# Second cross attention: two head pairs per output product with values as weights, sums of keys on GpSimd, maxima in a bank of their own

## The reference, cut to what matters

```python
def _L1_xattn_ref(x, y, Wq, Wk, Wv, Wp, bp):
    # x: layernorm of the rows (8, 64, 512), y: ctx_1024 (8, 1601, 512), H, D = 16, 32
    q = (x @ Wq.T).reshape(B, N, H, D)
    k = (y @ Wk.T).reshape(B, L, H, D)
    v = (y @ Wv.T).reshape(B, L, H, D)
    attn = jnp.einsum('bnhd,blhd->bhnl', q, k)
    attn = jax.nn.softmax(SCALE * attn, axis=-1)
    out = jnp.einsum('bhnl,blhd->bnhd', attn, v).reshape(B, N, C)
    return out @ Wp.T + bp
```

## Time and profile before

| | us |
|---|---|
| median of 3 runs | 1368.89 (1365.0 to 1373.93) |
| the profiled execution | 1376.89 |
| its span in the trace | 1375.2 |

### The profile page before, as it was taken

How to read it: one execution, slowest core, us unless ns; L and a number is a source line. 1 busy time by engine, 2 the same in 40 slices (tenths; PEclk the granted TensorE clock), 3 DMA queues, 4 the chain that set the end, 5 groups by cost and what they waited for, 6 DMA issues and landing times.

```text
span 1375.2 us, 34061 instructions
## 1 busy us (share of the span) xinstructions
PE 1227.7 (89%) x15423; PEld 924.7 (67%) x15424; DVE 616.3 (45%) x985; ACT 433.8 (32%) x822; POOL 70.4 (5%) x47
## 2 busy tenths in 40 slices
PE   7789888887999999999999999999999999756886
PEld 3334433685887887887887887787787788444773
DVE  2011387544224444444453454455445444544276
ACT  1010252232323343343334324334333333112332
POOL 0000000140000000000000000000000000701022
PEclk9899989899999999999999999999999999855999
DMA  9989850531020000010011010001001001300000
GB/s 355 380 354 389 306 209 28 218 113 51 16 79 20 21 33 32 17 52 32 17 53 33 17 52 32 17 21 64 17 21 62 18 21 35 129 2 1 16 2 31
DMA packets 38875, 115.67 MB, mean 84 GB/s; under 512 B 2504, under 2 KB 3016, under 8 KB 34640
## 3 DMA queue, kind: packets, MB, share of 16 engines
q1 hardware_dynamic: 38736, 113.50, 22.9%
HBM read 112.44 MB, written 1.05 MB: 83 GB/s over the span
## 4 chain that ended last, share of the span: by engine, by line
PE 70%; DVE 14%; issue 5%; SPq 5%; DMA 3%; ACT 3%; POOL 0%; DVEq 0%; ACTq 0%
PE SB L346 40%; PE SB L1052 7%; PE SB L337 5%; PE SC L1022 4%; SPq L501 4%; DVE LN L1331 4%; PE SB L1034 2%; DVE low L1316 2%; DMA R<-in_ctx_t 2%; PE SB L861 2%; DMA R<-in_ctx 1%; PE SB L929 1%; PE SB L330 1%; PE SC L837 1%; DVE Z L1347 1%
## 5 line engine op out<-in xcount | busy, mean ns | idle before, releaser
L346 PE MATMUL SB<-high,whigh 128*128 128x512 f32 (+2 forms) x512 | 186.6, 365 | 13.9 <-DVE low L1316 10.8
L1536 ACT COPY R<-SB 64x512 f32<-64x512 f32 (+1 forms) x240 | 118.5, 494 | 222.3 <-PE SB L346 220.2
L1331 DVE TENSOR_REDUCE LN<-SC 128x64 f32<-128x768 f32 x128 | 116.4, 951 | 152.4 <-PE SC L1022 152.4
L346 PE MATMUL SB<-high,wlow 128*128 128x512 f32 (+2 forms) x512 | 179.9, 351 | 0.0
L346 PE MATMUL SB<-low,whigh 128*128 128x512 f32 (+2 forms) x512 | 179.5, 351 | 0.0
L346 PE MATMUL SB<-whigh,high 128*128 128x512 f32 (+1 forms) x416 | 168.9, 406 | 0.0
L1347 DVE TENSOR_TENSOR Z<-SC,LN 128x768 f32<-128x768 f32 x128 | 116.6, 952 | 116.6 <-ACT LN L1562 116.6
L346 PE MATMUL SB<-whigh,low 128*128 128x512 f32 (+1 forms) x416 | 164.1, 395 | 0.0
L346 PE MATMUL SB<-wlow,high 128*128 128x512 f32 (+1 forms) x416 | 163.8, 394 | 0.0
L1566 ACT ACTIVATE Z<-Z 128x768 f32<-128x768 f32 (+1 forms) x192 | 120.9, 662 | 65.6 <-DVE Z L1347 64.4
L1052 PEld LDWEIGHTS SB<-R,Z 128*64 128x64 f32 (+1 forms) x3328 | 109.4, 145 | 17.0 <-issue 11.7
(11 more groups left out here) (213 smaller groups left out, 1394.5 us busy)
## 6 DMA issues: line engine op xcount, KB each, us to landing
R<-in_ctx_t SPq DMA_DIRECT2D x32, 1024.0 KB, 8.4
R<-in_ctx SPq DMA_DIRECT2D x8, 3072.0 KB
R<-in_ctx_t SPq DMA_DIRECT2D x16, 644.0 KB, 6.7
R<-in_f SPq DMA_DIRECT2D x4, 2048.0 KB, 15.8
R<-in_f SPq DMA_DIRECT2D x1, 8192.0 KB, 25.4
R<-in_ctx_t SPq DMA_DIRECT2D x12, 512.0 KB, 4.2
R<-in_Wk SPq DMA_DIRECT2D x3, 1024.0 KB, 10.1
R<-in_Wv SPq DMA_DIRECT2D x3, 1024.0 KB, 13.2
```

The source lines that it names most:

```text
L346: last = pe.matmul(out_, lhs[a][:, k, :], rhs[b][:, k, :], start=k == 0 and i == 0, stop=k == NC - 1 and i == 2)
L1331: inc(dve.tensor_reduce(tops[:, r * T:(r + 1) * T], sc_head[:, :, r, 0:6 * T].rearrange("p g (a q) -> p q g a", q=T), AX.XY, ALU.max), "ha ...
L1536: last = act.copy(keys[nu][64 * half:64 * half + 64, pairs, first * P:first * P + full], src[:, :, 0:full])
```

## The change

Two pairs share one step `o`: the values of a head (128 keys by 32) are the weights and the probabilities (64 columns) are streamed, the four heads of the two pairs going to the four groups of 32 columns of the array and the partitions of `BK[3]`. The column of ones is gone. There are two buffers of probabilities. GpSimd adds the 13 tiles of each pair in five instructions, and a new step `z` multiplies the sums by a 128 by 32 block of ones, so that they stand beside the outputs. DVE takes the reciprocal of 128 by 256 elements behind the last `z` of a batch and multiplies straight into `ot`; step `c` is gone. `m` and `b` use bank 2 alone, so jobs have a ring of two. A job may be cut in parts (`p`) so that given amounts of job work stand at each place; the last three value jobs of a batch (`w`) move into the batch that uses them, an `h` moves up to four jobs ahead. GpSimd's work for the fifth stage stays behind its sums in its stream.

```diff
+def attention(jobs, filled_out=True):
+    jobs, order, begun = list(jobs), [], 0
+    def split():
+        for job in jobs[:4]:
+            if job[0] == "h":
+                order.append(job)
+                jobs.remove(job)
+    def fill(us):
+        nonlocal begun
+        while us > 0 and jobs:
+            kind, x = job = jobs[0]
+            if kind in "kvw":
+                count = 12 * len(x[1]) if kind == "k" else 12
+                each = piece_n(x[0], 1) / 512 * 0.232 if kind == "k" else 0.232
+                if begun + math.ceil(us / each) < count:
+                    begun += math.ceil(us / each)
+                    order.append(("p", (job, begun)))
+                    return
+                us -= (count - begun) * each
+            elif kind != "h":
+                us -= 2.8
+            order.append(jobs.pop(0))
+            begun = 0
+    fill(1.2)
     for pr in range(HP):
+        outputs = [("o", pr // 2 - 1)] if pr and pr % 2 == 0 else []
+        order.append(("s", pr))
+        if not filled_out:
+            order += outputs
+        fill(3.2)
+        order.append(("m", pr))
+        if filled_out and outputs:
+            order += outputs
+        else:
+            fill(0.9)
+        order.append(("b", pr))
+        order += [("z", g) for _, g in outputs]
+        split()
+        fill(4.5 if pr == HP - 1 else 5.2 if outputs else 4.3)
+    order.append(("o", HP // 2 - 1))
+    fill(2.2)
+    order.append(("z", HP // 2 - 1))
+    return order + jobs
+LATE4 = [("w", t) for t in piece_tiles(KC - 1)]
+EARLY4 = projections()[:-len(LATE4)]
+FIRST4 = [("h", 0), ("q", 0)] + EARLY4
+BATCH4 = [("h", 0)] + attention(LATE4 + EARLY4)
+LAST4 = attention(LATE4 + [("y", 0), ("y", 1), ("y", 2)], False)
+RING4 = 2
 def numbered(steps, first=0):
-    jobs = [x for x in steps if x[0] not in "sohq-"]
+    jobs = [x for x in steps if x[0] not in "sohq-mbpz"]
...
-        VW = HD + 1
-        KW, VALS = HP * HK, KT_N * H * VW
+        KW, VALS = HP * HK, CTXW
         batch4 = KW + VALS
         keys = [view(u * batch4, KW, HP, HK) for u in range(2)]
-        vals = [view(u * batch4 + KW, VALS, KT_N, H * VW) for u in range(2)]
-        by_head4 = [v.rearrange("p t (h d) -> p t h d", d=VW) for v in vals]
+        vals = [view(u * batch4 + KW, VALS, KT_N, D) for u in range(2)]
...
-        p4 = Z[:, 1, 0:13 * P]
-        p4_half = [p4[:, g * HK:(g + 1) * HK].rearrange("p (r a q) -> p r a q", r=2, q=T) for g in range(2)]
-        p4_short = p4[0:MR, 2 * HK:2 * HK + P]
+        p4 = Z[:, 1, 0:KT_N * P], LN.rearrange("p a d -> p (a d)")[:, 0:KT_N * P]
...
+                if c == KC - 1:
+                    at, before = at4(BATCH4, b)
+                    n, k = at[LATE4[-1]]
+                else:
+                    at, before = at4(FIRST4 if isinstance(b, int) and b == 0 else BATCH4, b - 1)
+                    n, k = at["v", piece_tiles(c)[-1]]
...
-            for u in range(2):
-                inc(pool.memset(by_head4[u][:, :, :, HD:VW], 1.0), "ones4")
+            inc(pool.memset(ones, 1.0), "ones4")
+            inc(pool.nop(), "sums4", 2)
+            with pool.Fori(0, B) as b:
+                for pr in range(HP):
+                    w, n, exps = pr % 2, 32 * b + 4 * pr, 24 * b + 3 * pr
+                    pool.wait_ge(sem("e4"), exps + 2)
+                    inc(pool.tensor_tensor(added[:, :], p4_flat[w][0], p4_flat[w][1], ALU.add), "added4")
+                    pool.wait_ge(sem("added4"), n + 1)
+                    inc(pool.tensor_tensor(added_halves[:, :, 0:3, :], added_halves[:, :, 0:3, :],
+                                           added_halves[:, :, 3:6, :], ALU.add), "added4")
+                    pool.wait_ge(sem("added4"), n + 2)
+                    inc(pool.tensor_tensor(added_halves[:, :, 0, :], added_halves[:, :, 0, :],
+                                           added_halves[:, :, 1, :], ALU.add), "added4")
+                    pool.wait_ge(sem("added4"), n + 3)
+                    pool.wait_ge(sem("z4"), 4 * b + pr // 2 + 1)
+                    inc(pool.tensor_tensor(sums[w], added_halves[:, :, 0, :], added_halves[:, :, 2, :], ALU.add),
+                        "added4")
+                    pool.wait_ge(sem("added4"), n + 4)
+                    pool.wait_ge(sem("e4"), exps + 3)
+                    inc(pool.tensor_tensor(sums[w][0:MR], sums[w][0:MR],
+                                           p4_short[w].rearrange("p (r q) -> p r q", q=T), ALU.add), "sums4")
             at, before = at4(LAST4, B - 1)
             pool.wait_ge(sem("qb"), B)
-            for n in range(RING4):
-                pool.wait_ge(sem(f"full4_{n}"), before)
+            for late in LATE4[-RING4:]:
...
+                def some(job, n):
+                    (kind, x), first = job, begun.get(job, 0)
+                    c, ecs = x if kind == "k" else (piece_of(x), (0,))
+                    if first == 0:
+                        if kind == "k" and ecs[0] == 0:
+                            pe.wait_ge(sem("split"), KC * nxt + c + 1)
+                        bank4(job)
+                    begun[job], bk = n, BK[at[job][0]]
+                    for i, ec in enumerate(ecs):
+                        within = range(max(first - 12 * i, 0), min(n - 12 * i, 12))
+                        if within and kind == "k":
+                            m = piece_n(c, 1)
+                            last = three_products(bk[:, i * m:(i + 1) * m], 0, slice(ec * P, (ec + 1) * P), c,
+                                                  slice(0, m), True, within)
+                        elif within:
+                            m, at_ = min(P, MP - x * P), (x - PIECE_TILE[c]) * P
+                            last = three_products(bk[0:m, :], 1, slice(0, D), c, slice(at_, at_ + m), False, within)
+                    return last
...
+                        done4(job, some(job, 12 * len(x[1])))
+                    elif kind in "vw":
+                        done4(job, some(job, 12))
...
-                        bk = bank4(job)
                         pe.wait_ge(sem("tops4"), 8 * b + x + 1)
-                        done4(job, pe.transpose(bk[:, 0:P], tops, ident[:, :]))
+                        inc(pe.transpose(BK[2][:, 0:P], tops, ident[:, :]), "turned4")
                     elif kind == "b":
-                        bk = bank4(job)
-                        n, k = at["m", x]
-                        pe.wait_ge(sem(f"read4_{n}"), before + k + 2)
-                        done4(job, pe.matmul(bk[:, 0:P], mx[:, x:x + 1].to_broadcast([P, P]), ident[:, :],
-                                             start=True, stop=True))
+                        pe.wait_ge(sem("mx4"), 8 * b + x + 1)
+                        inc(pe.matmul(BK[2][:, 0:P], mx[:, x:x + 1].to_broadcast([P, P]), ident[:, :],
+                                      start=True, stop=True), "spread4")
                     elif kind == "o":
                         if x == 0:
-                            pe.wait_ge(sem("ones4"), 2)
                             pe.wait_ge(sem("o4_read"), b + 1)
-                            for n in range(RING4):
-                                pe.wait_ge(sem(f"read4_{n}"), before + 1)
+                            for late in LATE4[-RING4:]:
+                                n, k = at[late]
+                                pe.wait_ge(sem(f"read4_{n}"), before + k + 2)
                         for t in list(range(0, 4)) + [8, 9] + list(range(4, 8)) + [10, 11, 12]:
                             m = tile_keys(t)
                             if t in (0, 4, MF):
-                                pe.wait_ge(sem("e4"), 24 * b + 3 * x + {0: 1, 4: 2, MF: 3}[t])
-                            for r in range(2):
+                                pe.wait_ge(sem("e4"), 24 * b + 6 * x + 3 + {0: 1, 4: 2, MF: 3}[t])
+                            for j in range(4):
+                                w, r = j // 2, j % 2
                                 if t < MF:
                                     g, a = at_half(t)
-                                    weights = p4_half[g][:, r, a, :]
+                                    probabilities = p4_half[w][g][:, r, a, :]
                                 else:
-                                    weights = p4_short[:, r * T:(r + 1) * T]
-                                last = pe.matmul(sums4[r * T:(r + 1) * T, x, :], weights,
-                                                 by_head4[u][0:m, t, 2 * x + r, :], start=t == 0, stop=t == MF)
-                        if x == HP - 1:
-                            inc(last, "pv4")
-                    elif kind == "c":
-                        pe.wait_ge(sem("o4_read"), b + 2)
-                        bk = bank4(job)
-                        for k in range(2):
-                            last = pe.transpose(bk[:, k * P:(k + 1) * P], on4[:, k * P:(k + 1) * P], ident[:, :])
-                        done4(job, last)
```

(42 more changed lines are left out.)

118 lines of the change are left out of this document (46 added, 72 removed).

## The result

| | us |
|---|---|
| changed kernel, median of 19 runs | 1377.32 (1370.46 to 1385.84) |
| kernel before, median of 19 runs beside them | 1370.94 (1365.0 to 1383.4) |
| ratio, with its 95% interval | 1.0044 [1.0023, 1.0065] |
| profiled execution after, and its span | 1385.84, 1384.1 |

The change costs some 6 us where 7 were forecast as a gain. The profiled execution of the changed kernel is the slowest of its 19, so its trace shows somewhat more than the usual loss: between the two traces the span grew by 8.9 us. Two versions further down had one execution each in a slower state of the chip (1955.87 and 1476.4 us); medians and ratios are those of their other executions.

The account below looks back on a forecast made before the run. PE was taken to bound the kernel, busy 104.8 of 109.1 us per batch. Batches -13, clock +3.5, first projections -6.4, last batch -5 and tail +14 made -7, so 1362 us from a median of 1368.9; range 1350 to 1376.

Parts of the forecast that it names:

- Output products: PE's step o in the batches: 1.6 to 1.7 us for two pairs in place of 3.28, 6.7 less per batch.
- two turns: Rival on PE's output products: four column groups take two turns, 0.118 us a step; 1411 us in all, chance 0.05.
- exposed weight loads: Rival on PE's output products: weight loads don't hide, 26 x 0.027 x 32 = 22 us; 1384 us in all, chance 0.08.
- Waits: PE's waits in a batch: all 4.3 us go, new ones of 7.9 come, 3.6 us more than before.
- -6.7, +1.3 and -0.1: PE's work per batch in us: output products gain 6.7, the new z costs 1.3, dropping c gives back 0.1.
- The clock: PE's half-speed time behind two waits near 3 us: +0.5 per batch, +3.5 us in all, bounds -8 and +12.
- slower, by the clock: Second rival listed: each of four waits of 1.2 us and more halves PE's clock; 36 us more, 1398 us, chance 0.10.
- GpSimd's sums: GpSimd's additions, 4.3 us per pair beside a period of 12: hidden except at the end; DVE's splits lose nothing, at most 1.7 each.
- First projections: Stretch of PE alone before the batches: three value jobs leave, -8.4, and some waits come in; -6.4 us.
- Last batch: Last batch up to its last b, output products leaving the chain: -5 us, bounds -9 and 0.
- The tail: Last b to q5: GpSimd's fifth-stage work starts later and holds DVE's normalizations; +14 us, bounds +3 and +16.
- cleaner gain: First rival listed: DVE slips between GpSimd's instructions, waits halve, the clock never falls; 1332 us or so, chance 0.22.

Follow-up runs that it names:

- the written-out kernel before: Kernel before the change, with PE's seven equal batches written out instead of a hardware loop of two batches: 1375.12 us, ratio 1.0025.
- all three edits: Changed kernel with GpSimd's fifth-stage work between the last sums, PE's batches written out and ACT's copies reordered: 1308.61 us, ratio 0.9548 against the kernel before.
- Moving it alone in the kernel before: Kernel before with one more wait, so GpSimd's fifth-stage work starts only behind the last output product: 1387.51 us, ratio 1.0129.
- the fillers and the loop kept: Changed kernel, PE's loop kept, with unused matmuls in the waits before v8 and k(3,3): 1351.95 us, ratio 0.9851 against the kernel before.
- the experiment on the additions: GpSimd's additions per pair cut from five to two small ones: 1361.06 us on the changed kernel with written-out batches, 1336.42 us with useless matmuls added too.

## Why the prediction was wrong

**Output products: right.** 1.59 us for 1.6 to 1.7. Loads of 32 columns and streams of 64 ran at 0.06 us a step of four, so the rivals of two turns (0.118) and of exposed weight loads (0.059 + 0.027 = 0.086) fall. With the second falls the rule of the Trainium skill, "TensorE: Matmul & The Clock Gate", section "Part 3: Packing small matmuls", that a load overlaps matmuls in flight only when its row group differs: all rows are used here, and by 1.59 us for 104 instructions the trace disagrees.

**Waits: right without the clock.** 7.7 us per batch were left (22.3 + 16.3 + 15.2 over seven), forecast 7.9, at the jobs and for the engines named. PE's busy time at full clock fell by 6.9 per batch (723.71 us over seven batches in the written-out kernel before, 675.70 with all three edits), where -6.7, +1.3 and -0.1 make -5.5. The further 1.4 I can't place. From these the batches should have gained 24 us (7 x 3.5), more than my 13.

**The clock: wrong, and the main failure.** The step that failed was "two waits near 3 us instead of one of 1.6", of which I took "one and a bit, +0.5 per batch, +3.5", with bounds of -8 and +12. Half-speed time rose by 41 us (17.1 to 58.0). At 0.46 that is about 19 us, at the lowest price measured, 0.34, it is 14. Both lie outside my bounds, which counted one drop of one length per wait; some were twice as long, and others came behind the loop's gaps. The rival "slower, by the clock" had the mechanism: it needed 2.9 us a batch beyond my figure to decide, and 2.2 came ((19 - 3.5) / 7).

**The loop's return: missing.** No step and no rival has it. 9.4 us of gaps, 9.8 with the clock behind them where nothing else drops it. Before, `issue` stood for 0.3 us in these batches. What differs at the jump is in the text of the change: before, its first jobs were keys that waited for DVE's split; now the value jobs `w` stand there, ready at once, with `z`'s eight short instructions ahead. That PE's instructions are fetched too late for them fits this and the written-out kernels, but no trace shows the fetch; which of the two makes the difference was not tried. What is shown is that the gaps belong to the return: they go when the batches are written out, and the kernel before gains nothing by it.

**GpSimd's sums: wrong.** "I take nothing, at most 1.7 each": they hold up DVE's splits, 2279 ns for 1820, and cost 6.8 us in the batches, of which the waits `m` 0 and `m` 2 carry 5.8. My 1.2 us for each of the two waits held this by luck, which is why the sum of the waits was still right.

**First projections: right.** -7.0 for -6.4. **Last batch: its size off,** -8.4 for -5, inside the bounds (-9 and 0).

**The tail: right in mechanism, short in size.** The forecast ends of the first three normalizations, b + 15.6, 18.0 and 23.1, came at b + 15.7, 17.7 and 22.3. The fourth was put at 36.4 and ended at 38.9, since the memset behind the addition held it too: +18.8 for +14, outside the +16 I gave as a bound. Moving the work gave 15.9 us back and bears it out. Moving it alone in the kernel before cost 16.3 by the median, of which the one trace shows 8.0 in the tail.

**The sum.** Beyond the forecast went the clock 15, the loop 9, the tail 5 and the untouched front 3; short of it stayed PE's work 10, the last batch 3, the waits and the first projections 2. That is +17, or +12 with the clock at the lower price, where the span missed by 15.9 (-7 forecast, +8.9 measured). The two largest misses are terms that a list of waits in the kernel before does not show: what a wait does to the clock behind it, and what a loop's return costs once the work around it is short. Either of them, taken away alone, turns the loss into a gain: 1351.95 us with the fillers and the loop kept, 1361.28 with the batches written out and no fillers.

The cleaner gain of 1332 us that I gave 0.22 is no property of the change but of its order: with ACT's copies in another place alone it is 1342.

Slips in the sums of the prediction decided nothing. A clock that never falls is worth 7 x 1.7 = 12 us, where the bound has -8 and the first rival takes -5; with the 12 that rival comes to 1321. The second rival counts its 5.1 us a batch from 1.7, where the sum has 2.2; from there it is 32 us more, 1394.

## What to carry to other kernels

Price a wait on PE as its length and what the clock loses behind it, by counting half-speed time in the trace and not by one drop per wait; and where a change's time looks inexplicable, put useless matmuls into the wait, which takes the clock out of the comparison (the experiment on the additions read 0.2 us without that and 11.4 with it). When a stream gains an item on a helping engine, look at what stands behind it in that engine's queue: moving GpSimd's fifth-stage work between the sums was worth 15.9 us, more than twice the gain that was forecast for the whole change. Before a loop's end is filled with short ready work, ask what covered its jump.

## What the runs showed of the hardware

- In the tail a TENSOR_SCALAR from SBUF ended within 0.3 us behind the end of the GpSimd instruction it met, and one was held through two in a row: 7.23 us for 0.55. A start 1.3 us earlier escaped it.
- A subtraction on DVE with two SBUF inputs waited for the addition under way on GpSimd and then took about its own time (3.13 us for 2.28); the next addition waited for it (2.39 us for 0.45). DVE's reads of PSUM were not lengthened (951 and 952 ns).
- PE's loop return left 2.62 + 2.56 and 1.86 + 2.32 us of gaps in one kernel and single ones of 3.8 and 3.9 in another with the same loop; in the kernel before, with value matmuls ahead of it, all idle time put to issue was 0.3.
- The same waits in a batch gave 23.9 us of half speed in seven batches with a period of 105.9, and 58.0 with slightly shorter waits before the maxima: the loss depends on more than the wait's length. By what, I leave open.
- Four column groups of 32, with loads and streams in all of them, take 0.06 us a step of four at full clock.
